# Output projection of a pair of tiles in seven block products instead of eight

## The reference

```python
q = heads(x @ Wq + bq); k = heads(x @ Wk + bk); v = heads(x @ Wv + bv)
scores = jnp.einsum('bhqd,bhkd->bhqk', q, k) * scale
scores = jnp.where(mask[:, None] == 0, -jnp.inf, scores)
attn = jax.nn.softmax(scores, axis=-1)
out = jnp.einsum('bhqk,bhkd->bhqd', attn, v)
out = out.transpose(0, 2, 1, 3).reshape(b, s, D_MODEL)
y = out @ Wo + bo
return _layernorm(x + y, axis=-1)
```

## Time and profile before

| | us |
|---|---|
| median of 3 runs | 821.98 (821.61 to 822.32) |
| profiled execution, its own time | 821.39 |
| its span, first to last instruction | 819.5 |
| TensorE busy in it | 812.0 |
| VectorE busy | 544.9 |
| GpSimd busy | 512.6 |
| ScalarE busy | 238.2 |

### The profile page before, as it was taken

How to read it: one execution, slowest core, us unless ns; L and a number is a source line. 1 busy time by engine, 2 the same in 40 slices (tenths; PEclk the granted TensorE clock), 3 DMA queues, 4 the chain that set the end, 5 groups by cost and what they waited for, 6 DMA issues and landing times.

```text
span 819.5 us, 25422 instructions
## 1 busy us (share of the span) xinstructions
PE 812.0 (99%) x11286; PEld 665.1 (81%) x11286; DVE 544.9 (66%) x691; ACT 238.2 (29%) x315; POOL 512.6 (63%) x407
## 2 busy tenths in 40 slices
PE   9999999999999999999999999999999999999997
PEld 7788888888888888888888888888888888888886
DVE  5667667766567666676665776656766567766795
ACT  6532233221332222332223322133322233223223
POOL 1386667656675565856658566576665767657682
PEclk9999999999999999999999999999999999999999
DMA  9224424253342433424334243352424434234342
GB/s 321 90 79 122 120 81 135 84 143 95 88 143 72 149 92 92 139 70 142 105 91 134 71 144 95 82 154 82 128 88 106 136 82 131 84 108 118 105 105 104
DMA packets 50173, 92.37 MB, mean 113 GB/s; under 512 B 11280, under 2 KB 13328, under 8 KB 47888
## 3 DMA queue, kind: packets, MB, share of 16 engines
q1 hardware_dynamic: 47568, 87.08, 36.2%
q10 hardware_dynamic: 2496, 3.67, 1.6%
HBM read 40.37 MB, written 16.78 MB: 70 GB/s over the span
## 4 chain that ended last, share of the span: by engine, by line
PE 98%; DVE 1%; POOL 0%; ACT 0%; issue 0%; POOLq 0%; DVEq 0%
PE ring L289 23%; PE ring L291 21%; PE ring L290 21%; PE ring L386 7%; PE ring L387 7%; PE ring L390 7%; PE psum_s L357 6%; PE ring L375 6%; PE ring L407 1%; PE ring L309 0%; POOL soft L912 0%; PE ring L313 0%; PE ring L317 0%; DVE soft L717 0%; DVE top L724 0%; ACT soft L568 0%
## 5 line engine op out<-in xcount | busy, mean ns | idle before, releaser
L912 POOL TENSOR_TENSOR soft<-soft,top 128x1024 f32<-128x1024 f32 x62 | 125.2, 2020 | 77.5 <-DVE top L724 77.5
L171 POOL TENSOR_TENSOR soft<-soft,inverse 128x1024 f32<-128x1024 f32 x62 | 118.9, 1918 | 24.9 <-DVE inverse L731 22.2
L563 ACT ACTIVATE kt<-ring,bk 128x512 f32<-128x512 f32 x64 | 43.6, 681 | 258.7 <-PE ring L291 258.6
L889 POOL TENSOR_TENSOR x_lo<-x_raw,x_hi 128x512 fp32r<-128x512 f32 x56 | 72.0, 1286 | 61.1 <-ACT x_hi L548 61.1
L289 PE MATMUL ring<-wv_hi,x_hi 128*128 128x512 f32 x256 | 103.5, 404 | 0.0
L289 PE MATMUL ring<-x_hi,wk_hi 128*128 128x512 f32 x256 | 103.1, 403 | 0.0
L728 DVE TENSOR_REDUCE total<-soft 128x16 f32<-128x1024 f32 x62 | 75.6, 1219 | 41.0 <-ACT soft L568 41.0
L291 PE MATMUL ring<-wv_hi,x_lo 128*128 128x512 f32 x256 | 100.1, 391 | 0.0
L291 PE MATMUL ring<-x_hi,wk_lo 128*128 128x512 f32 x256 | 99.9, 390 | 0.0
L290 PE MATMUL ring<-x_lo,wk_hi 128*128 128x512 f32 x256 | 99.7, 390 | 0.0
L290 PE MATMUL ring<-wv_lo,x_hi 128*128 128x512 f32 x256 | 99.6, 389 | 0.0
(11 more groups left out here) (81 smaller groups left out, 1362.3 us busy)
## 6 DMA issues: line engine op xcount, KB each, us to landing
pt<-soft SPq DMA_DIRECT2D x464, 64.0 KB, 2.0
x_raw<-in_xt SPq DMA_DIRECT2D x15, 1024.0 KB, 6.8
row<-in_x SPq DMA_DIRECT2D x60, 256.0 KB, 2.7
out_rows<-row SPq DMA_DIRECT2D x60, 256.0 KB, 2.6
adj<-in_adj SPq DMA_DIRECT2D x16, 128.0 KB, 2.9
pt<-soft ACTq DMA_DIRECT2D x32, 64.0 KB, 2.2
kt<-in_wk SPq DMA_DIRECT2D x4, 256.0 KB, 5.1
row<-in_wv SPq DMA_DIRECT2D x1, 1024.0 KB, 8.4
```

Source lines behind the costliest of these rows:

```text
L171: ops.tensor_tensor(soft_of(c), soft_of(c), on_keys(inverse[:, c % 2, :]), ALU.mult).then_inc(normed, 1)
L889: nc.gpsimd.tensor_tensor(x_lo[:, buf, :, rows], x_raw[:, :, rows], x_hi[:, buf, :, rows].bitcast(F32), ALU.subtract).then_inc(x_lo_done, 1)
L912: nc.gpsimd.tensor_tensor(soft_of(c), soft_of(c), on_keys(top[:, c % 2, :]), ALU.subtract).then_inc(centred, 1)
```

## The change

For the first 27 pairs (54 tiles, `PLAIN`) the output projection of a pair is seen as a product of two-by-two blocks. Rows: tile 0 or 1 of the pair. Inner side: features 0 to 255 or 256 to 511. Columns of Wo: left or right half. Instead of the eight block products of `project_out` for both tiles there are seven, by Winograd's form of Strassen's algorithm. Each block product is six matmuls of 256 columns (two chunks, three parts).

- At the start, four sums of blocks of Wo are made on GpSimd (`add_weights`) and split into `t_hi` (ScalarE) and `t_lo` (VectorE).
- For each pair, ScalarE copies the mixed rows to SBUF as they are (`ot_raw`, in the place of `pt` buffer 1), then makes `ot_hi` from that (`read_pair`). VectorE makes four sums of blocks of rows (`s_raw`, in `v`), and `ot_lo` in two parts, of which one block (tile 1, first half) is no longer needed. ScalarE and GpSimd split the sums into `s_hi` and `s_lo` (`split_sums`).
- TensorE makes `first_products` between `project_v(a)` and `project_v(b)`, `middle_products` at the end of the turn, and `last_products` behind the scores of the next turn.
- VectorE adds the products into the rows in six instructions (`add_first`, `add_middle`, `add_last`) in place of two `add_y`; the row sums come four tiles back, and the normalisation of these rows goes from VectorE to ScalarE (`norm_by_act`), with `make_shift` on GpSimd.
- To make room, `pt` has two buffers instead of four, the mask bias is kept once (256 elements a group instead of 1024), and `mask` is two instructions of 512 elements instead of one of 1024. `place(c)` waits for the mix of tile `c - 2` instead of `c - 4`. Rows are loaded at the end of SP's turn.

```diff
-        pt = sb("pt", [P, 4, 2, HEADS, SQ])
+        pt = sb("pt", [P, 2, 2, HEADS, SQ])
+        s_hi = sb("s_hi", [P, 4, 2, P], F32R)
+        s_lo = sb("s_lo", [P, 4, 2, P], F32R)
+        t_hi = sb("t_hi", [P, 4, 2, HALF], F32R)
+        t_lo = sb("t_lo", [P, 4, 2, HALF], F32R)
-        bias = sb("bias", [P, 2, GT, 2, KC, SQ])
+        bias = sb("bias", [P, 2, GT, 2, SQ])
...
+            def product(out, left_hi, left_lo, right_hi, right_lo, adds=False):
+                for kc in range(2):
+                    nc.tensor.matmul(out, left_hi[:, kc, :], right_hi[:, kc, :], start=kc == 0 and not adds, stop=False,
+                                     skip_group_check=adds)
+                    nc.tensor.matmul(out, left_hi[:, kc, :], right_lo[:, kc, :], start=False, stop=False,
+                                     skip_group_check=adds)
+                for kc in range(2):
+                    last = nc.tensor.matmul(out, left_lo[:, kc, :], right_hi[:, kc, :], start=False, stop=kc == 1,
+                                            skip_group_check=adds)
+                return last
...
+            def first_products(m):
+                pe.wait_ge(masked, 4 * (m + 2))
+                pe.wait_ge(ot_hi_done, m + 1)
+                pe.wait_ge(ot_lo_first, m + 1)
+                pe.wait_ge(ot_lo_done, m + 1)
...
+                product(first_bank()[:, 0:HALF], *rows_block(0, 1), *weights_block(1, 0))
+                product(first_bank()[:, HALF:D], *rows_block(1, 1), *weights_sum(4)).then_inc(y_part, 1)
+                product(ring[:, 2, 0:HALF], *rows_block(0, 0), *weights_block(0, 0)).then_inc(y_part, 1)
+
+            def middle_products(m):
+                pe.wait_ge(s_hi_done, m + 1)
+                pe.wait_ge(s_lo_done, m + 1)
+                product(ring[:, 3, 0:HALF], *rows_sum(1), *weights_sum(1)).then_inc(y_part, 1)
+                pe.wait_ge(row_part, PARTS * m + P1)
+                product(ring[:, 2, 0:HALF], *rows_sum(2), *weights_sum(2), adds=True).then_inc(y_part, 1)
+
+            def last_products(m):
+                pe.wait_ge(row_part, PARTS * m + P6)
+                product(ring[:, 2, 0:HALF], *rows_sum(3), *weights_sum(3), adds=True).then_inc(y_part, 1)
+                product(ring[:, 3, 0:HALF], *rows_sum(4), *weights_block(1, 1), adds=True).then_inc(y_part, 1)
...
                 score(a)
                 score(b)
+                if p >= 2:
+                    last_products(p - 2)
...
                 project_v(a)
+                first_products(p - 1)
                 pe.wait_ge(q_done, b + 5)
                 project_v(b)
-                pe.wait_ge(ot_lo_done, p)
-                project_out(a - 2)
-                project_out(b - 2)
+                middle_products(p - 1)
...
+            def read_pair(m):
+                act.wait_ge(mixed, 2 * m + 2)
+                nc.scalar.copy(ot_raw().rearrange("p t c (g q) -> p (t c) g q", g=2),
+                               mixed_rows(m, slice(0, 2))).then_inc(ot_raw_done, 1)
+                act.wait_ge(ot_raw_done, m + 1)
+                wait_for(act, y_part, PARTS * (m - 1) + P1)
+                nc.scalar.copy(ot_hi[:, :, :, :], ot_raw()).then_inc(ot_hi_done, 1)
+
+            def split_sums(m):
+                act.wait_ge(s_raw_done, 4 * (m + 1))
+                nc.scalar.copy(s_hi[:, :, :, :], s_raws(m)).then_inc(s_hi_done, 1)
...
+            def split_blocks(m):
+                dve.wait_ge(ot_hi_done, m + 1)
+                nc.vector.tensor_tensor(ot_lo[:, 0], ot_raw()[:, 0], ot_hi[:, 0].bitcast(F32),
+                                        ALU.subtract).then_inc(ot_lo_first, 1)
+                nc.vector.tensor_tensor(ot_lo[:, 1, 2:4, :], raw_block(1, 1), ot_hi[:, 1, 2:4, :].bitcast(F32),
+                                        ALU.subtract).then_inc(ot_lo_done, 1)
+
+            def add_rows(m):
+                dve.wait_ge(ot_raw_done, m + 1)
+                done = 4 * m
+                nc.vector.tensor_tensor(s_raw(m, 2), raw_block(0, 0), raw_block(1, 0), ALU.subtract).then_inc(s_raw_done, 1)
+                nc.vector.tensor_tensor(s_raw(m, 0), raw_block(1, 0), raw_block(1, 1), ALU.add).then_inc(s_raw_done, 1)
+                split_blocks(m)
+                dve.wait_ge(s_raw_done, done + 2)
+                nc.vector.tensor_tensor(s_raw(m, 1), s_raw(m, 0), raw_block(0, 0), ALU.subtract).then_inc(s_raw_done, 1)
+                dve.wait_ge(s_raw_done, done + 3)
+                nc.vector.tensor_tensor(s_raw(m, 3), raw_block(0, 1), s_raw(m, 1), ALU.subtract).then_inc(s_raw_done, 1)
```

The loop of VectorE and that of GpSimd, changed:

```diff
             for p in range(FULL):
                 a, b = 2 * p, 2 * p + 1
-                if p >= 2:
-                    add_row(a - 3)
                 mask(a)
                 mask(b)
+                if p == 0:
+                    split_weight_sums()
+                sum_up(a)
                 if p >= 2:
-                    norm_row(dve, nc.vector, a - 3)
-                sum_up(a)
+                    add_last(p - 2)
                 sum_up(b)
                 turn(a)
+                if p >= 2:
+                    row_sums(a - 4)
+                if p >= 1:
+                    add_rows(p - 1)
                 turn(b)
+                read_v(a)
                 if p >= 1:
-                    split_ot(p - 1)
-                read_v(a)
+                    add_first(p - 1)
+                if p >= 2:
+                    row_sums(b - 4)
                 read_v(b)
                 if p >= 1:
-                    add_row(a - 2)
-                    norm_row(dve, nc.vector, a - 2)
+                    add_middle(p - 1)
...
             for p in range(FULL):
                 a, b = 2 * p, 2 * p + 1
-                if p >= 2:
-                    make_rstd(a - 3)
                 centre(a)
                 centre(b)
                 normalise(pool, nc.gpsimd, a)
                 normalise(pool, nc.gpsimd, b)
-                add_bo(a)
+                if p >= 1:
+                    add_bo(a - 2)
+                    add_bo(b - 2)
+                if p >= 2:
+                    make_shift(a - 4)
+                if p >= 1:
+                    split_sums(p - 1)
+                if p >= 2:
+                    make_shift(b - 4)
                 if p % 2 == 0:
                     make_bias(p // 2 + 1)
                 for c in (a, b):
                     if c + 2 * GT < TILES:
                         split_x(c + 2 * GT)
-                add_bo(b)
-                if p >= 1:
-                    make_rstd(a - 2)
```

More of the change, by code:

```diff
@@ L178, in by_chunk, with ot_raw, raw_block, s_raws @@
             return ot[:, tiles, :, :].rearrange("p t c (g q) -> p (t c) g q", g=2)
+        def ot_raw():
+            return pt[:, 1].rearrange("p q h k -> p (q h k)").rearrange("p (t c n) -> p t c n", t=2, c=KC)
+        def raw_block(i, j):
+            return ot_raw()[:, i, 2 * j:2 * j + 2, :]
+        def s_raws(m):
+            return v[:, 2 * m % 4:2 * m % 4 + 2, :].rearrange("p t (n c q) -> p (t n) c q", n=2, c=2)
+        def s_raw(m, n):
+            return s_raws(m)[:, n]
+        def w_raw_block(i, j):
+            return w_raw[3][:, 2 * i:2 * i + 2, j * HALF:(j + 1) * HALF]
+        def t_raw(n):
+            return pt[:, n // 2, n % 2, :, :].rearrange("p h k -> p (h k)").rearrange("p (c n) -> p c n", c=2)
+        def quarter(m, i, j):
+            return row[:, (2 * m + i) % 4, j * HALF:(j + 1) * HALF]
+        def first_bank():
+            return psum_s[:, 0].rearrange("p t b c k -> p (t b c k)")
         def ot_count(c):
@@ new lines, in rows_block, with weights_block, rows_sum, weights_sum @@
+            def rows_block(i, j):
+                return ot_hi[:, i, 2 * j:2 * j + 2, :], ot_lo[:, i, 2 * j:2 * j + 2, :]
+            def weights_block(i, j):
+                columns = slice(j * HALF, (j + 1) * HALF)
+                return w_hi[3][:, 2 * i:2 * i + 2, columns], w_lo[3][:, 2 * i:2 * i + 2, columns]
+            def rows_sum(n):
+                return s_hi[:, n - 1], s_lo[:, n - 1]
+            def weights_sum(n):
+                return t_hi[:, n - 1], t_lo[:, n - 1]
+            def first_products(m):
[3 more added lines that the diff above has]
+                pe.wait_ge(ot_lo_done, m + 1)
+                if m == 0:
+                    pe.wait_ge(w_hi_done, 4 * KC)
+                    pe.wait_ge(w_lo_done, 4 * KC)
+                    pe.wait_ge(t_hi_done, 4)
+                    pe.wait_ge(t_lo_done, 4)
+                product(first_bank()[:, 0:HALF], *rows_block(0, 1), *weights_block(1, 0))
+                product(first_bank()[:, HALF:D], *rows_block(1, 1), *weights_sum(4)).then_inc(y_part, 1)
+                product(ring[:, 2, 0:HALF], *rows_block(0, 0), *weights_block(0, 0)).then_inc(y_part, 1)
@@ L465, in _ @@
             score(T - 7)
+            last_products(PAIRS - 6)
             pe.wait_ge(v_done, T - 9)
@@ L638, in _ @@
             split_w(3, 3)
+            for n in range(4):
```

(23 more changed lines are left out.)

151 lines of the change are left out of this document (95 added, 56 removed).

## The result

The changed kernel takes 836.77 us (median of 4 runs, 833.57 to 837.88), the kernel before 822.15 beside it (4 runs, 821.61 to 823.01). The ratio is 1.017, with a 95% interval of 1.014 to 1.0201: slower by 14.6 us where I had said 6. The profiled execution took 837.44 us with a span of 835.6, near the top of the four; what follows is read from that one execution and from the one of the kernel before.

The account below looks back on a forecast made before the run. PE was taken to bound the kernel. Per pair -0.40 + 0.05 + 0.61 = +0.26, times 27 is +7.0, plus 0.4 at the start, on 821.39: 828.8, taken as 828.0 us; range 821.5 to 838.

Parts of the forecast that it names:

- What PE saves: Output projection of a pair: 42 matmuls of 256 columns take 5.04 us against 5.44, saving 0.40 a pair.
- contention: Product matmuls in the loop: 0.05 us more a pair, as some meet ScalarE and VectorE work.
- The Trainium skill's overlap rule: Product weight loads overlap only into another row group; otherwise 7.9 us instead of 5.04, total 905; chance 0.02.
- The wait at `first_products`: Chain behind the mix: first product 0.50 us late plus 0.11 restart, 0.61 a pair, outlasting the saving; chance 0.63.
- upper bound: Wait at `first_products`: 0.95 us with a 1.24 copy, no overlap of subtractions and 0.05 more from semaphore to start.
- The turn: Main loop: about 25.4 us (25.16 before), PE gap of about 0.5 before the first product, ended by `split_blocks`' second subtraction.
- the term of the start: Weight sums beside projections at the start: the later first turn may cost up to 1 us, taken as 0.4.
- The masks' cover: SP's transfers behind `turn(b)` land at 427.5, before the next mask(b) at about 428.2: no cost.
- A second wait behind the first: GpSimd's `s_lo`, or x_lo in every second turn, late: 0.3 to 0.8 us more a pair, 836 to 850; chance 0.13.
- the tail: End of the kernel: its order changes little, costed at 0.

Follow-up runs that it names:

- e1: Changed kernel with `ot_hi` made tile by tile and each product waiting for its own block alone: 823.47 us beside 822.91, ratio 1.0004.
- e3: Changed kernel with `split_weight_sums` moved ahead of the first masks: 835.16 us, turn 1 26.66 and turn 2 27.11.
- e4: Changed kernel with GpSimd's `add_bo` of turns 1 and 2 between the two `centre`: 834.06 us, turn 1 26.83 instead of 29.66.
- e7: Changed kernel with the edits of e1, e3 and e4 together: 817.93 us beside 822.64 for the kernel before, ratio 0.9945.
- e6: Changed kernel with GpSimd's `make_shift` ahead of `add_bo` in every turn: 851.13 us, 25.96 a turn.
- m1_port: Separate kernel, output zeros, timing VectorE beside GpSimd: two-SBUF-input additions of 256 elements take 0.419 us alone, 1.486 beside GpSimd's addition of 1024 elements.

## Why the prediction was right and wrong

The direction, and the turn of the main loop, were right; the time was 9 us short, 6.7 of it because of the start.

- **What PE saves.** Forecast 42 x 0.120 = 5.04 us of products a pair, plus 0.05 of contention, against 5.44. The 42 take 5.21 without waits (e1), but not by contention: nearly all start 0.12 apart there too. The rest is in two places, the last product ahead of the scores (0.21 to their start) and the first one behind them (0.22 to its next), and the kernel before pays as much at both (0.32 and 0.34 instead of 0.23), and the 5.44 counts neither. PE behind the scores, before and after:

```profile
426.88 0.50 PE L289 MATMUL ring<-x_hi,wk_hi 128*128 128x512 f32 x1
427.22 0.39 PE L290 MATMUL ring<-x_lo,wk_hi 128*128 128x512 f32 x1
```
```profile
436.82 0.39 PE L447 MATMUL ring<-t_hi,s_hi 128*128 128x256 f32 x1
437.04 0.28 PE L449 MATMUL ring<-t_lo,s_hi 128*128 128x256 f32 x1
```

  Counted alike, the 42 take 5.02, and a pair saves 0.42: this term was right, and the 0.05 was nothing. The weight loads do overlap: neighbours start 0.12 apart, each with its own. The Trainium skill's overlap rule, weighed in the prediction, doesn't hold for them.
- **The wait at `first_products`.** Forecast 0.50 + 0.11 = 0.61, measured 0.55 + 0.07 = 0.62. The parts differ more than the sum: copies 1.02 and 1.05 as taken, but from VectorE's end to PE's start 0.15 us, not the 0.05 of the earlier trace rows (last section; the prediction had this only in its upper bound), and a shorter restart. e1 shows that the wait and nothing else turned the saving into a loss.
- **The turn.** Forecast about 25.4 with a gap of 0.5 ended by the second subtraction; measured 25.45 with a gap of 0.39 idle, ended by it in 26 of 27. 7.0 was forecast for the 27 turns, 7.7 came. The scores take 0.07 longer a turn (from their first start to what follows 1.59 in the median, 1.52 before), which was in no term; the mix stays at 1.41. So -0.42 + 0.62 + 0.07 = +0.27, against 0.28 measured.
- **The step that failed** is the term of the start, "the later first turn may cost up to 1 us. I take 0.4". It measured 7.1. It rested on "VectorE four subtractions 2.5 us", which took 4.20 because GpSimd's `centre` ran beside them; and behind it stood, without a word, that VectorE's new instructions cost the same whatever GpSimd does. The work that hid them was the work that held them: 1.7 us in those four, 2.6 of the wait in turn 1, and the wait of turn 2, where L891 and L892 take 1.00 and 1.51; the 1.5 of the clock followed from the wait. Undoing one or the other (e3, e4) takes 3.0 or 2.8 us off turn 1, both with e1 take 4.7 of the 7.1 away.
- **The sign that was there.** The kernel before has the lock once, outside the rows that I used. The prediction took 689 ns a subtraction from the group that writes `wo_lo`; the same instruction for `wv_lo` averages 890, the first of the four 1.52 us, beside GpSimd's first `make_bias`:

```profile
L783 DVE TENSOR_TENSOR wv_lo<-row,wv_hi 128x512 fp32r<-128x512 f32 x4 | 3.3, 890 | 4.7 <-ACT wv_hi L605 4.7
```
- **The masks' cover.** In turns 1 and 2 of the changed kernel the masks wait for the transfers out of `soft` (6.4 us in 3 waits), which I had weighed with the times of a steady turn alone. That this lengthens the start isn't shown: the kernel before has one such wait of 2.4 us, e7, the fastest, has six of 8.0 together, and in turn 1 of the changed kernel VectorE came to `add_rows` only 0.2 us after `ot_raw` was there.
- **A second wait behind the first.** None came in the loop: `s_lo` took 2.42 (forecast 1.92 to 2.6) and ended at 432.95, 0.7 before PE at 433.69; no turn waited for x_lo. This cover held, as did the tail (0.2).
- **The margin that was not seen.** In the loop the same lock lay 0.2 us from the chain. e6 shows the price of losing it: 14 us, 0.51 a turn.

What isn't settled: how the 2.4 us of e7's start divide. Not tried was a version in which VectorE subtracts straight from PSUM, as the kernel before does; m1_port has an instruction with one PSUM input at 0.41 us beside GpSimd's additions.

## What to carry to other kernels

When a change adds VectorE instructions with two SBUF inputs, lay GpSimd's timeline beside theirs, in the first turns as well as in a steady one: what overlaps there may not run beside it but wait. Saved matmul time is worth what the shortest chain of small steps behind it leaves; here one wait of 0.6 us ate a saving of 0.3 (a turn of 25.17 before, 24.88 in e1), and waiting block by block gave it back. A per-turn sum says nothing of turns 0 to 2, so cost these from their own rows.

## What the runs showed of the hardware

- The lock doesn't need two inputs on GpSimd's side. In m1_port, VectorE's additions beside GpSimd's `tensor_scalar` of 1024 elements with one input took 1.25 us each, three in a row, with GpSimd's at 1.10 to 1.21. DVE and POOL of m1_port; the DVE row also covers the time before 33.6, when GpSimd still did additions:

```profile
28.32 9.07 DVE L65 TENSOR_TENSOR d_with_pool_ts<-left,right 128x256 f32<-128x256 f32 x6
```
```profile
26.28 7.30 POOL L86 TENSOR_TENSOR p_a<-pleft,pright 128x1024 f32<-128x1024 f32 x3 [3.21 <-ACT a_out L97]
33.67 3.45 POOL L84 TENSOR_SCALAR p_b<-pleft 128x1024 f32<-128x1024 f32 x3
```

- It isn't always held for the whole of GpSimd's instruction. `rstd` of one element per partition runs from 426.46 to 427.30 in the rows above, and L891 and L892 beside it (426.45 and 426.79) take 0.43 and 0.42 us. In the kernel before, `make_bias` from int32 runs from 18.47 to 22.12; of the four subtractions from 18.54 on the first takes 1.52, the other three 0.68 each.
- How soon PE starts behind a wait doesn't go by the engine that it waited for. It was 0.05 us after ScalarE's end in the earlier trace rows, and also after a VectorE one, the changed kernel's first (1.38 to 1.44). It was 0.15 after L884 in 26 of the 27 turns (428.56 to 428.71), and also after a ScalarE cast (8.81 to 8.95). In the cases of 0.15 the trace has PE's queue pass an instruction that only waits (428.60 to 428.65), in those of 0.05 the weight load itself waits. In turn 1, where more semaphores are asked for, it was 0.31.
- Small matmuls have gaps that the trace puts down to issue and to no semaphore. The matmuls of `score(a)` and `score(b)` together, 128 by the trace and not the 256 of the section on the kernel (the mix is 128 too), take 1.59 before (at 425.36) and 1.68 after (at 435.21), and once 2.7, with a hole of 0.88. PE's timeline after:

```profile
537.13 1.54 PE L409 MATMUL psum_s<-kt,qt 32*64 32x64 f32 x122
539.55 0.34 PE L409 MATMUL psum_s<-kt,qt 32*64 32x64 f32 x6 [0.88 <-issue]
```

PE's sequencer was through with the last wait ahead of a score 4.0 to 4.1 us before it began in the kernel before, and 1.8 to 2.0 us in the changed one. That less lead makes the holes is only argued: no run changed it alone.
